# Beside expert steps, attention's matmuls first in a tile, the step's behind them, and the residual at the tile's end

## What is computed

```python
def xattn(q, enc, W_kv, b_kv, W_out, b_out, heads):      # 16 heads of 16 channels
    kv = (enc @ W_kv.T + b_kv).reshape(B, S, heads, d_k, 2)
    k, v = kv[..., 0], kv[..., 1]
    scores = einsum('bshd,bstd->bsht', qh, k) / sqrt(d_k)  # within one token: heads against heads
    context = einsum('bsht,bstd->bshd', softmax(scores), v)
    return context @ W_out.T + b_out
def ffn(x, gate_w, w1, w2):                              # 8 experts, hidden 1024
    probs = softmax(einsum('ntd,ed->nte', x, gate_w))
    g, m = top_k(probs.transpose(0, 2, 1), 64)           # each expert takes 64 of 256 tokens
    h = gelu(einsum('nekd,edf->nekf', x[batch, m], w1))
    out[batch, m] += g[..., None] * einsum('nekf,efd->nekd', h, w2)
x = x + tanh(g_xattn) * xattn(layernorm(x), ctx, ...)
x = x + tanh(g_ffn) * ffn(layernorm(x), ...)
```

## Time and profile before

| | us |
|---|---|
| median of 3 runs | 736.58 |
| range of the runs | 736.11 to 738.33 |
| the profiled execution | 736.63 |
| its span in the trace | 734.6 |
| mean granted clock of PE | 0.928 |

### The profile page before, as it was taken

The page is one execution under the profiler, slowest core; times in us unless marked ns, Lnnn a source line. Parts: engine busy times, 40 slices in busy tenths (PEclk is TensorE's granted clock), DMA queues, the critical chain, the costliest instruction groups (busy, mean ns, idle before and its releaser), DMA issues.

```text
span 734.6 us, 10843 instructions
## 1 busy us (share of the span) xinstructions
PE 641.7 (87%) x3592; PEld 514.2 (70%) x3592; DVE 619.9 (84%) x726; ACT 434.1 (59%) x1077; POOL 550.1 (75%) x497
## 2 busy tenths in 40 slices
PE   5668786654799999997999999979999999999994
PEld 2334333322678888775888888758888889999994
DVE  4999999999999999889999999899999461577762
ACT  5477767643577777855777777657776533233320
POOL 3888888888868888698888887888888625445534
PEclk9988898655699999998999999989999999999997
DMA  6967774322367778766887777577777868999972
GB/s 177 345 231 259 263 242 188 125 99 75 123 182 247 237 230 231 224 201 175 243 237 230 230 237 231 185 218 206 235 229 219 268 174 271 317 308 314 308 217 29
DMA packets 97068, 160.90 MB, mean 219 GB/s; under 512 B 8171, under 2 KB 74486, under 8 KB 97014
## 3 DMA queue, kind: packets, MB, share of 16 engines
q1 hardware_dynamic: 84150, 142.91, 58.9%
q0 software_dynamic: 12288, 16.79, 12.1%
q10 hardware_dynamic: 576, 0.52, 0.2%
HBM read 126.63 MB, written 33.55 MB: 218 GB/s over the span
## 4 chain that ended last, share of the span: by engine, by line
PE 55%; DVE 21%; DMA 9%; issue 7%; POOL 6%; ACT 2%; POOLq 0%; ACTq 0%; DVEq 0%
PE bank L1017 20%; PE bank L998 20%; DVE prod_v L459 9%; DMA out_dram<-ys,ids 7%; DVE co L461 5%; PE bank L925 5%; DVE S L461 4%; PE bank L945 3%; POOL prod_p L313 2%; PE bank L986 2%; PE bank L908 2%; DMA xg<-xn_scratch,ids 1%; POOL tree_a L319 1%; POOL out_dram L379 1%; PE bank L957 1%
## 5 line engine op out<-in xcount | busy, mean ns | idle before, releaser
L998 PE MATMUL bank<-xin,w1in 128*128 128x256 f32 x1536 | 206.4, 292 | 7.6 <-issue 4.7
L998 PEld LDWEIGHTS bank<-xin,w1in 128*128 128x128 f32 x1536 | 195.8, 198 | 9.1 <-issue 8.7
L1017 PE MATMUL bank<-w2s,hT 128*128 128x256 f32 x768 | 175.4, 382 | 0.0
L379 POOL DMA_INDIRECT out_dram<-ys,ids x64 | 110.0, 1719 | 76.2 <-ACT ys L748 57.8
L1017 PEld LDWEIGHTS bank<-w2s,hT 128*128 128x128 f32 x768 | 142.4, 190 | 17.8
L738 ACT ACTIVATE hT<-bank 128x512 f32<-128x512 f32 x128 | 76.5, 598 | 117.9 <-PE bank L998 117.5
L461 DVE TENSOR_REDUCE co<-prod_v 128x208 f32<-128x3328 f32 (+2 forms) x32 | 109.7, 3428 | 1.1
L459 DVE TENSOR_TENSOR prod_v<-bank,Ex 128x3328 f32<-128x3328 f32 (+2 forms) x32 | 109.5, 3423 | 0.1
L313 POOL TENSOR_TENSOR prod_p<-kvs,q 128x1024 f32<-128x1024 f32 (+2 forms) x32 | 94.6, 2955 | 14.5 <-ACT q L706 14.5
L459 DVE TENSOR_TENSOR prod_v<-bank,q 128x3072 f32<-128x3072 f32 (+2 forms) x32 | 98.1, 3066 | 6.6 <-ACT q L706 6.6
L461 DVE TENSOR_REDUCE S<-prod_v 128x192 f32<-128x3072 f32 (+2 forms) x32 | 98.2, 3070 | 1.1
(11 more groups left out here) (123 smaller groups left out, 1079.9 us busy)
## 6 DMA issues: line engine op xcount, KB each, us to landing
w1in<-w_parts SPq DMA_DIRECT2D x128, 512.0 KB, 5.6
w2s<-in_L_ffn_w_dram SPq DMA_DIRECT2D x32, 1024.0 KB, 6.1
w_parts<-w1s SPq DMA_DIRECT2D x32, 512.0 KB, 3.5
w1raw<-in_L_ffn_w_dram SPq DMA_DIRECT2D x32, 256.0 KB, 4.4
ct<-in_ctx_dram SPq DMA_DIRECT2D x32, 128.0 KB, 4.5
xt<-in_x_dram SPq DMA_DIRECT2D x32, 128.0 KB, 4.6
out_dram<-x SPq DMA_DIRECT2D x32, 128.0 KB, 4.3
xn_scratch<-xn SPq DMA_DIRECT2D x32, 128.0 KB, 2.8
```

What stands on the lines that cost most here:

```text
L379: pool.indirect_dma_start(out=out_rows[:, :], out_offset=bass.IndirectOffsetOnAxis(ap=ids[:, g % 2, p * E + e:p * E + e + 1], axis=0), in_ ...
L998: ins = pe.matmul(HB[k % 2][:, D * f:D * (f + 1)], w1in[:, k, w, c, P * f:P * (f + 1)].bitcast(f32r), xin[:, n % 2, x_, c, :], start=(m == ...
L1017: ins = pe.matmul(dst, hT[:, n % 2, f, cols], w2s[:, n % 2, f, :], start=(f == 0), stop=(f == FC - 1))
```

## The change

Some tiles are called relaxed: behind tile 11, not a routing tile and not the one after one (12 to 17, 20 to 25, 28 to 31).

- **PE, all tiles with a step:** con's transposes, keys and values and the output projection come ahead of hidden parts 0 and 1. In a relaxed tile the token transposes come ahead of them too, right behind the contexts'.
- **PE, around a routing tile:** in the tile before it the logits stand between hidden parts 2 and 3, outputs(n - 1, 0) comes last, and outputs(n - 1, 1) is put off into the routing tile. There the probabilities' transposes come first of all, then the put-off outputs; the lists' matmul stands behind hidden part 3 and ahead of both halves of outputs.
- **ScalarE:** gelus 0 and 1 behind the exponentials and xn, the token copy early in relaxed tiles, `make_q` ahead of the xn transposes' copy. Before a routing tile the logits' copy, gelu 3, a table load ahead of time and the gate's exponentials stand ahead of the x2 statistics, and the ys are put off with their outputs.
- **VectorE, relaxed tiles:** `low_tokens` of the next step takes the residual's place behind Sc, and the residual goes to the end, ahead of the reciprocal and con.
- **GpSimd, routing tiles:** `rsqrt` behind the first instruction of `scores` instead of ahead of it.

```diff
+    relaxed = lambda s: s > N0 and not routing(s) and not routing(s - 1)
@@ gpsimd, share
                 pool.tensor_tensor(pv, in0, in1, ALU.mult).then_inc(prodp_s, 1)
+                if root is not None:
+                    rsqrt(root)
@@ vector, tile
-                if t > 0:
+                if relaxed(t):
+                    low_tokens(t - N0 + 1)
+                elif t > 0:
                     residual(t - 1)
...
-                if 0 <= t - N0 + 1:
+                if relaxed(t):
+                    residual(t - 1)
+                elif 0 <= t - N0 + 1:
                     low_tokens(t - N0 + 1)
@@ scalar, a routing tile
                 if routing(s):
+                    if n >= 1:
+                        take_y(n - 2)
                     if n >= 0:
                         take_ctT(s + 1)
-                        gelu(n, 0)
-                        gelu(n, 1)
                     take_coT(s - 1)
                     take_kv(s + 1)
                     make_xn(s - 2)
+                    if n >= 0:
+                        gelu(n, 0)
+                        gelu(n, 1)
+                    take_xnT(s - 2)
                     x_stats(s + 2)
-                    take_xnT(s - 2)
+                    make_q(s + 1)
                     if n >= 0:
                         gelu(n, 2)
+                    take_logits(s - 2)
+                    if n >= 0:
                         gelu(n, 3)
-                    take_logits(s - 2)
-                    make_q(s + 1)
@@ scalar, the others
-                gelu(n, 0)
-                gelu(n, 1)
+                if relaxed(s):
+                    take_xh(n + 1)
                 take_coT(s - 1)
...
                 exponentials(s)
-                take_xh(n + 1)
                 make_xn(s - 2)
+                gelu(n, 0)
+                gelu(n, 1)
+                if not relaxed(s):
+                    take_xh(n + 1)
                 if s + 2 < NT:
                     x_stats(s + 2)
+                if s + 1 < NT:
+                    make_q(s + 1)
                 take_xnT(s - 2)
                 gelu(n, 2)
-                gelu(n, 3)
-                take_logits(s - 2)
-                if s + 1 < NT:
-                    make_q(s + 1)
+                if routing(s + 1):
+                    take_logits(s - 2)
+                    gelu(n, 3)
+                    act.activation(exp_warm[:, :], tanh_g[:, 0:1], ACT.Exp)
+                    gate_exp(s // TG - 1)
+                else:
+                    gelu(n, 3)
+                    take_logits(s - 2)
                 x2_stats(s - 1)
-                if routing(s + 1):
-                    gate_exp(s // TG - 1)
-                if n >= 1:
+                if n >= 1 and not routing(s + 1):
                     take_y(n - 1)
@@ tensor
+                if routing(s):
+                    prob_transposes(s // TG - 1)
+                    if n >= 1:
+                        outputs(n - 2, 1)
                 if n >= 0 and s + 1 < NT:
                     ctx_transposes(s + 1)
...
+                if relaxed(s):
+                    token_transposes(n + 1)
                 co_transposes(s - 1)
...
                 project_out(s - 1)
-                if not routing(s):
+                if n >= 0:
+                    hidden(n, 0)
+                    hidden(n, 1)
+                if not relaxed(s) and not routing(s):
                     token_transposes(n + 1)
-                if n >= 1:
-                    outputs(n - 1, 0)
-                xn_transposes(s - 2)
-                if n >= 0:
+                if routing(s) or routing(s + 1):
+                    xn_transposes(s - 2)
+                    if n >= 0:
+                        hidden(n, 2)
+                    logits(s - 2)
+                    if n >= 0:
+                        hidden(n, 3)
+                    if routing(s):
+                        route_columns(s // TG - 1)
+                    if n >= 1:
+                        outputs(n - 1, 0)
+                        if routing(s):
+                            outputs(n - 1, 1)
+                    if routing(s):
+                        token_transposes(n + 1)
+                else:
+                    if n >= 1:
+                        outputs(n - 1, 0)
+                    xn_transposes(s - 2)
                     hidden(n, 2)
                     hidden(n, 3)
-                logits(s - 2)
...
+                    logits(s - 2)
+                    if n >= 1:
+                        outputs(n - 1, 1)
```

More of the change, by code:

```diff
@@ L307, in _, with share @@
         def _(pool):
-            def share(heads, in0, in1, dst, n_tree, done):
+            def share(heads, in0, in1, dst, n_tree, done, root=None):
                 full = [P, heads, DK, DK]
@@ L343, in scores @@
                     pool.wait_ge(Sc_ready, t)
-                share(H - hk, Kv, qi, S[:, hk * DK:H * DK], 2 * t, Sp_done)
+                share(H - hk, Kv, qi, S[:, hk * DK:H * DK], 2 * t, Sp_done, t + 1 if routing(t) else None)
             def values(t):
@@ L418, in _ @@
             for s in range(NT):
-                if routing(s):
-                    rsqrt(s + 1)
                 scores(s)
@@ L1072, in _ @@
                 n = s - N0
+                if routing(s):
+                    prob_transposes(s // TG - 1)
+                    if n >= 1:
+                        outputs(n - 2, 1)
                 if n >= 0 and s + 1 < NT:
                     ctx_transposes(s + 1)
-                if routing(s):
-                    prob_transposes(s // TG - 1)
-                if n >= 0:
-                    hidden(n, 0)
-                    hidden(n, 1)
+                if relaxed(s):
+                    token_transposes(n + 1)
                 co_transposes(s - 1)
@@ L1083, in _ @@
                 project_out(s - 1)
-                if not routing(s):
+                if n >= 0:
+                    hidden(n, 0)
+                    hidden(n, 1)
+                if not relaxed(s) and not routing(s):
                     token_transposes(n + 1)
-                if n >= 1:
-                    outputs(n - 1, 0)
-                xn_transposes(s - 2)
-                if n >= 0:
+                if routing(s) or routing(s + 1):
[17 more added lines that the diff above has]
+                    xn_transposes(s - 2)
                     hidden(n, 2)
                     hidden(n, 3)
-                logits(s - 2)
-                if routing(s):
-                    route_columns(s // TG - 1)
-                if n >= 1:
-                    outputs(n - 1, 1)
-                if routing(s):
-                    token_transposes(n + 1)
+                    logits(s - 2)
+                    if n >= 1:
+                        outputs(n - 1, 1)
             n = n1 - 1
```

## The result

The changed kernel takes 745.75 us (median of 4 runs, 744.55 to 747.22) where the kernel before takes 737.46 beside it on the same chip: a ratio of 1.0108, 95% interval 1.0071 to 1.0145. It is slower by 8.3 us. The profiled execution took 745.55 us with a span of 743.6, 9.0 more than before.

What follows compares the result with a forecast made beforehand. PE was taken to bound the plain tiles, with VectorE a close second. Relaxed tiles +7.0, first tiles +1.1 and routing tiles -0.9 gave +7.2 us on 736.63: 743.8 us, range 735 to 749.

Steps and rivals of the forecast that it cites:

- The relaxed tiles: Tiles 12 to 16, 20 to 24, 28 to 31: projection waits for ScalarE's ctT, +0.5 us a tile, +7.0 us.
- The first tiles: Tiles 11 and 12: PE waits for con, then on ScalarE's row; +1.1 us, bounds -1 to +2.
- two waits told for tile 12: PE in tile 12 waits about 1.3 us before the third hidden part and 0.5 us before the logits.
- The passages: Tile 17's start to tile 20's, and around tile 26: -0.9 us together, bounds -8.7 to +5.
- The steps up to con: From tile 17's start: logits 11.4, gsum 15.5, lists' matmul about 31.6, con 43.2 us, with PE idle 3.6 us.
- the sentence that keeps the clock up: Around con's wait at the routing tiles: lower value kept, since the gap is shorter than today's three together.
- The rival of the clock: Clock falls to 1.2 GHz in con's wait, 1.7 to 2.3 us in two places: 748; chance 0.14, shared with worse ScalarE waits.
- VectorE's lead: VectorE runs ahead of PE in relaxed tiles until ScalarE's exponentials; worth something only where VectorE is the bound.
- the routing tiles pay: Lists' matmul, exponentials and tile 19 wait for nothing: 4.8 and 3.9 us gained, 736.0 us; chance 0.15.

Runs made afterwards that it cites:

- ctT first: The changed kernel with ScalarE copying the contexts (ctT) ahead of the two ys in relaxed and routing tiles: 741.70 us, 1.0050 to the kernel before.
- three edits: The changed kernel with ctT ahead of ys, xn transposes' copy early in tiles 17 and 25, token copy ahead of x2 statistics in routing tiles: 730.41 us.
- the best kernel: The changed kernel with ctT, xn transposes' copy and routing tiles' exponentials and lists' matmul earlier, con ahead of xin's low part: 728.29 us, 0.9861 to before.
- con first with the plain tiles old: The best kernel with the old order in plain tiles 12 to 16, 20 to 24 and 28 to 31: 728.81 us, 0.9885 to the kernel before.
- routing alone: The changed kernel with new orders only in tiles 11, 17 to 19 and 25 to 27, plain tiles in the old order: 741.35 us, 1.0043 to before.

## Why the prediction was right, and where it was not

The direction, the range and nearly the size were right: +7.2 us were forecast, +8.3 came between the medians and +9.0 between the spans. By its terms:

**The relaxed tiles, forecast +7.0, came to about +8.4.** Of the 14 tiles of this term eleven show 0.63 each in the table, tile 12 is counted at as much, and the stretch from tile 30 on (two of them and the tail) gave 0.84. Tiles 17 and 25 are relaxed too and stand in the passages. The mechanism was as told, to the row: the projection at T + 1.36 (forecast 1.37), put down to ScalarE's ctT. Across the kernel PE's waits for ctT are 8.4 us in 19 places, of which the kernel before has one, of 1.9 us, in its first tiles (PE's waits, us in total, times, longest; after, then before):

```profile
PE bank L941 <- ACT ctT L655: 8.4, 19, 1.9
```
```profile
PE bank L925 <- ACT ctT L650: 1.9, 1, 1.9
```

The size of a tile was short by 0.11, since I costed the projection itself as unchanged. It takes 1.92 us to its bias and not 1.81. The experiment with ctT first took 0.49 of the wait away (the projection starts at T + 0.87) and left the longer projection, 0.09 of the 0.13.

**The first tiles, forecast +1.1, came to +0.55** (1.18 by the table, less the 0.63 of tile 12 as a relaxed one). Of the two waits told for tile 12 the trace has neither; 0.97 us before the token transposes for the low part of xin and a stretch of low clock are there instead. Two such waits, 1.56 us for a gelu and 0.45 for the xn transposes' copy, stand one tile earlier, in tile 11, behind 3.27 us of waiting for con(10), and the forecast has none of the three. Tile 11 is even so 0.25 us shorter than before, where PE waited 2.84 and 1.50 us. The term is small, its waits were wrong, and its size was near by luck.

**The passages, forecast -0.9 together, came to +0.9** (with the other two +9.8, the loss from tile 11 on). The steps up to con were right: from tile 17's start the logits were told to wait till 11.4 (11.36), gsum for 15.5 (15.8), the lists' matmul for 31.6 (31.9), con for 43.2 (43.5), 3.6 us of idle PE (3.69), the projection for 43.9 (44.3), tile 20 for 63.1 (63.2). But the last of these is right by two errors that cancel. I had tile 19 wait 0.9 and 1.0 us for a gelu and the xn transposes' copy, and neither wait is there; and I kept the clock up, and it fell: from the projection behind the wait to the output projection it took 3.82 us and not 2.23. The two belong together. Where the clock stays up in the same tile (three edits), PE runs into the waits again, though for less than told, 0.46 us for the copy and some tenths for the gelu:

```profile
349.62 0.61 PE L978 MATMUL bank<-gwT,xnT 128*128 128x8 f32 x4 [0.46 <-ACT xnT L655]
```

From con's transposes to the next tile it is 18.47 us there and 19.22 in the changed kernel, so that of the 1.6 us at the low clock only 0.75 are left at the tile's end. Around tile 26 the same fall stood behind the logits' wait too, for another 1.6 us, and the forecast of 63.1 missed by that. The failed step is the sentence that keeps the clock up because one gap is shorter than three together. The rival of the clock had the right mechanism in the two waits for con, at 1.6 us instead of 1.7 to 2.3 in the matmuls behind the first; the third fall, behind the logits' wait in tile 25, it did not have. The Trainium skill ("TensorE: Matmul & The Clock Gate", section "Why this matters for your kernels") warns of idle gaps between bursts for that reason. The trace agrees with it in tiles 19 and 27, where the granted clock was 0.50 and 0.57 behind the wait, and I should have weighed it more. The length of the gap, 1.72 us in both, does not tell why the clock fell in tile 25 and not in tile 17.

**VectorE's lead** I had put at nothing in the plain tiles and at something undefined elsewhere. It is worth 2.6 and 1.0 us in the changed kernel's passages, with what the clock did in them, and 2.1 in each of the best kernel's.

**The rival "the routing tiles pay"** (4.8 and 3.9 us gained) was wrong for the change as it stands, but what it describes exists: with other orders in ScalarE's queue, con ahead of the low part on VectorE and the lists' matmul earlier on PE the passages fall to 57.7 us, 6.3 and 5.4 under the kernel before. Most of what stood between the change and its gain was work that PE waits for behind longer work in ScalarE's and VectorE's queues.

## What to carry to other kernels

When a block that covers a copy is moved away, look at what stands ahead of that copy in the in-order queue of the engine that makes it: here two instructions of 0.84 us together ahead of a 0.38 us copy made most of 0.63 us in each plain tile, and exchanging them gave 0.50 back. A wait in front of PE can cost more than it lasts when the clock falls behind it, so single repairs can look poor (4.0 and 2.8 us) where they bring 15.3 together with a third: try them together before dropping any. An exchange on one engine that needs its input earlier (the low part behind Sc) has to be made together with the move on the engine that makes this input.

## What the runs showed of the hardware

- **The clock after one wait is not the same each time.** Behind a wait of 1.72 us before the logits, with PE busy before and behind, the granted clock stayed at 1.00 in tile 17 of the changed kernel and fell towards 0.50, from the 2.4 GHz level to the 1.2 GHz level, in its tile 25 (0.54) and in tiles 17 and 25 of ctT first (0.60 and 0.50 in the stretch behind). The kernels' end shows it more sharply: the wait for the low part of w2 is 2.21 us in all eleven traces, with the same matmuls before and behind, and from the first to the last of the outputs behind it 7.07 to 7.42 us passed in nine of them and 6.06 and 6.07 in two (con first with the plain tiles old, and routing alone). Behind the 16 waits for con of 3.02 to 3.70 us, in tiles 11, 19 and 27, the projection was slow every time, 2.57 to 3.56 us to its bias. Behind shorter ones it was 1.82 (a wait of 2.83), 2.65 (2.48) and 1.81 twice (2.11). So the wait's length alone does not decide. What else does stays open.
- **A fall cost some 1.6 us in the matmuls behind it,** and less at the tile's end where the slower matmuls covered a wait (0.75 in tile 19): 12 hidden matmuls and 16 of the outputs took 2.13 and 4.44 us from start to start in tile 25 and 1.51 and 3.46 at full clock:

```profile
461.43 2.33 PE L1014 MATMUL bank<-xin,w1in 128*128 128x256 f32 x12
463.56 4.61 PE L1033 MATMUL bank<-w2s,hT 128*128 128x256 f32 x16
468.00 0.38 PE L980 MATMUL bank<-ident,pr 128*32 128x128 f32 x2
```

- **The projection takes 0.1 us more when its weights have only just been copied.** It took 1.92 us to its bias behind the awaited copy, 1.90 in ctT first, and 1.81 in the order before. The short block ahead, con's transposes, is the same in all three. What differs is the copy: in ctT first it ends at 241.40, the first weight load starts at 241.45 and the first matmul at 241.47. In tile 13 of the kernel before, and in tile 19 of three edits, the copy had long been done, the load started 0.11 us ahead of the matmul, and the block took 1.81 and 1.82. PE's weight loads, ctT first and then three edits:

```profile
241.45 0.30 PEld L943 LDWEIGHTS bank<-wkvT,ctT 128*128 128x128 f32 x2
```
```profile
335.31 0.30 PEld L946 LDWEIGHTS bank<-wkvT,ctT 128*128 128x128 f32 x2
```

So most of the 0.13 us that ctT first left may be the copy's too, since it comes only just in time there. That is read from the rows; no run took it apart.
